# A two-layer graph attention kernel: a new order on all engines, and the value bias rows as pairs of 32-row matmuls

## The chip, the cores and the metric

The kernel runs on one core of one Trainium2 chip. The time is the device time of one execution in microseconds (us). The kernel before took 2665.45 us in the median of 3 runs (2662.31 to 2666.25).

## What is computed

The input is `x` (128 graphs, 128 nodes, 256 features, fp32) and `adj` (128 x 128 x 128, int32). Two layers follow each other, each with 8 heads of 32 columns:

```
# layer 0
q, k = x @ Wq + bq, x @ Wk + bk
attn = softmax(q k^T / sqrt(32))
out  = sum over r in 0..3 of (attn * (adj == r)) @ (x @ Wv[r] + bv[r])
x    = ln(x + out @ Wo + bo) * g1 + beta1
x    = ln(x + gelu(x @ W1 + b1) @ W2 + b2) * g2 + beta2
# layer 1 (no biases on q, k, v)
e    = leaky(q k^T);  attn = softmax(where(adj > 0, e, -9e15))
out  = ln(attn @ v) * g1 + b1
out  = ln(concat(out, x) @ Wffn^T) * g2 + b2
return out + x
```

The value biases `bv[r]` (4 x 256 = 1024 numbers) are one of the two things that the change touches.

## The kernel before, in words

**Pairs.** Two graphs are worked on at a time, a pair: 64 pairs in all. Every product of two fp32 matrices is made of three fp16 products (high x high, high x low, low x high). So each operand is split by a copy on ScalarE (ACT) that makes the high part and a subtraction on VectorE (DVE) or GpSimd (POOL) that makes the low part.

**Stages of one pair on TensorE (PE).** Named by their functions: `transpose_x`, `queries_keys_0` (12 matmuls of 256 columns each for q and for k), `values_0` (four jobs `v0_0` to `v0_3`, each a bias matmul and 6 matmuls of 512 columns), `scores` of layer 0 (`s0`: 16 fp32 matmuls of 32 rows, four row groups of the array into four banks, recorded as 32), `transpose_edges`, `attend_0` for each graph (64 small matmuls), `transpose_attention_0`, `output_projection` (y0), `transpose_x1` (yT0), `hidden` (four jobs of 12 matmuls), `feed_forward` (f, 48 matmuls), `transpose_x2` (xT1), `queries_keys_1`, `scores` of layer 1 (`s1`: four 512-column matmuls that put the mask down, then 16 fp32 matmuls in row groups), `values_1` (v1), `attend_1`, `transpose_attention_1` (oT1) and `last_product` (w, 24 matmuls).

**The bias.** `bv_rows` has 128 partitions, all zero but two: row 0 holds the high part of all 1024 biases and row 32 the low part. In `values_0` (L473) one matmul of `ones16` (128 x 128) with 512 columns of `bv_rows` starts each of the four banks (L478), and the six products are added to it. That is four bias matmuls for each pair.

**The order.** It is written out by hand. Each engine has a function `steps(n)` (PE L599, ACT L802, DVE L1030, POOL L1187, and L403 for the DMA queue of SyncE) that `pipeline` calls for n = 0 to 68. In step n an engine does, in a fixed order, stages of several pairs: `hidden(n - 2, 0)` is the hidden layer of the pair two behind. Every engine goes strictly through its list; semaphores (one for each result, counting up) hold it where an input isn't there or a buffer isn't free. PE's list before begins with f(n-3), v1(n-4), y0(n-2), v0_1 and v0_2(n-1), w(n-5), xT1(n-3), v0_3(n-1), k1(n-3), yT0(n-2), edges(n-1), q1(n-3), the hidden jobs (n-2), and ends with xT0(n), attend_0(n-1, 0), s1(n-3), attend_1(n-4), attend_0(n-1, 1), q0, k0, v0_0 and s0(n), oT0(n-1), oT1(n-4). What follows calls the work between two such calls a step; a full step has all of them.

**Banks.** All results of PE go through the eight banks of PSUM. `PE_BANKS` (L29) gives in PE's order the job, its bank, its lag, and the semaphore that says that the bank has been read out. `bank_free` makes a job wait for the reader of the job before it in the same bank.

**DMA.** SyncE loads x and adj (adj twice), transposes the probabilities of both layers (`transpose_probs_0`, `transpose_probs_1`) and stores the result. The store reads `x2b`. POOL writes `x2b` twice for a pair: `residual_shift_1` (L1172) puts x2 + b2b there and `result` (L1180) adds the normed rows. `residual_shift_1(m)` waits until the store of pair m - 1 has landed (L1177), and in POOL's list before it comes soon behind the `result` of that pair, with two instructions between (L1114 and one L1151); behind it on POOL stand `hidden_low` 1 and 2, `rstd("o1")` and `attention_scaled_0`, for which PE's oT0 waits.

Of the kernel before, what the change touches and what calls it, by code (L numbers as in the profile page):

```python
# [6 lines left out]
F16 = mybir.dt.float16  # L7
# [6 lines left out]
P = 128  # L14
G = 2
# [13 lines left out]
PE_BANKS = [  # L29
    ("f", 2, 3, "f_added", 1, 1),  # L30
    ("v1", 1, 4, "v1_lo", 1, 1),
    ("y0", 7, 2, "y0_added", 1, 1),
    ("v0_1", 2, 1, "v0_lo", 4, 2),
    ("v0_2", 0, 1, "v0_lo", 4, 3),
    ("w", 3, 5, "w_normed", 1, 1),
    ("xT1", 7, 3, "xT1_lo", 1, 1),
    ("v0_3", 5, 1, "v0_lo", 4, 4),
    ("k1", 7, 3, "k1_sb", 1, 1),
    ("yT0", 4, 2, "yT0_lo", 1, 1),
    ("edges", 6, 1, "p0_masked", 4, 4),  # L40
    ("q1", 0, 3, "q1_sb", 1, 1),
    ("h_0", 4, 2, "h_gelu", 4, 1),
    ("h_1", 2, 2, "h_gelu", 4, 2),
    ("h_2", 5, 2, "h_gelu", 4, 3),
    ("h_3", 4, 2, "h_gelu", 4, 4),
    ("xT0", 7, 0, "xT0_lo", 1, 1),
    ("o0_0", 3, 1, "o0_added", 2, 1),
    ("s1_0", 2, 3, "s1_leaky", 4, 1),
    ("s1_1", 1, 3, "s1_leaky", 4, 2),
    ("s1_2", 4, 3, "s1_leaky", 4, 3),  # L50
    ("s1_3", 5, 3, "s1_leaky", 4, 4),
    ("o1_0", 6, 4, "o1_scaled", 2, 1),
    ("o1_1", 0, 4, "o1_scaled", 2, 2),
    ("o0_1", 7, 1, "o0_added", 2, 2),
    ("q0", 2, 0, "q0_sb", 1, 1),
    ("k0", 3, 0, "k0_sb", 1, 1),
    ("v0_0", 7, 0, "v0_lo", 4, 1),
    ("s0_0", 1, 0, "p0_lo", 4, 1),
    ("s0_1", 0, 0, "p0_lo", 4, 2),
    ("s0_2", 6, 0, "p0_lo", 4, 3),  # L60
    ("s0_3", 4, 0, "p0_lo", 4, 4),
    ("oT0", 3, 1, "oT0_lo", 1, 1),
    ("oT1", 5, 4, "oT1_affine", 1, 1),
# [27 lines left out]
def build(nc, a, out):  # L91
# [12 lines left out]
    with ExitStack() as ctx:  # L104
# [1148 lines left out]
```

## Time and profile before

| what | value |
|---|---|
| median of 3 runs | 2665.45 us |
| the profiled execution, first to last instruction | 2664.5 us |
| PE busy | 2484.1 us (93%) |
| ACT busy | 2271.1 us (85%) |
| DVE busy | 2100.7 us (79%) |
| POOL busy | 1914.5 us (72%) |
| mean granted clock of PE | 0.982 of full speed |

The span leaves out only what lies around the first and the last instruction; it is 0.95 us under the median. A busy share is that of the whole span, so it doesn't say what ends a wait. Matmuls are pipelined and their ends are modelled: of two neighbouring rows on PE, the difference of the starts is the measure. The rows of the timeline merge neighbouring instructions of one kind (x12 is twelve); a bracket gives idle time before the row and what ended it.

### The profile page before, as it was taken

What the parts mean: (1) busy time and instruction counts of PE and PEld (TensorE: products, weight loads), DVE (VectorE), ACT (ScalarE), POOL (GpSimd) and SP (SyncE); (2) the same over time, 40 slices, a digit from 0 to 9 for tenths busy, and PEclk for the clock granted to TensorE, in tenths of its full rate; (3) what the DMA queues carried; (4) which work ended last, traced back from release to release, by engine and by line L of the source; (5) the groups of instructions that cost most, each with busy time, mean ns of one, the idle gap of its engine ahead of it and who ended that gap; (6) DMA issues with size and microseconds to landing.
All of it is one profiled execution on the core that took longest, in us unless ns stands there. A gap on an engine that the chain in (4) does not pass through costs nothing.

```text
span 2664.5 us, 83008 instructions
## 1 busy us (share of the span) xinstructions
PE 2484.1 (93%) x31496; PEld 1991.9 (75%) x31496; DVE 2100.7 (79%) x3730; ACT 2271.1 (85%) x6226; POOL 1914.5 (72%) x2126
## 2 busy tenths in 40 slices
PE   2799999999999999999999999999999999999974
PEld 1577777778777777777777877877777777777763
DVE  4578888888888878878888888888888888787842
ACT  3588998998898888898899899889989988888963
POOL 1358778777777867777877777787777777677764
PEclk9899999999999999999999999999999999999986
DMA  4134424424433433433442443343344334244222
GB/s 130 33 57 89 75 59 89 83 60 80 89 68 66 89 68 66 89 68 66 89 83 56 84 89 65 69 89 74 60 89 83 65 75 83 54 86 83 57 55 44
DMA packets 610377, 196.72 MB, mean 74 GB/s; under 512 B 539072, under 2 KB 609216, under 8 KB 609984
## 3 DMA queue, kind: packets, MB, share of 16 engines
q1 hardware_dynamic: 606816, 188.01, 36.5%
q8 instruction: 254, 4.16, 0.7%
q10 hardware_dynamic: 3168, 3.41, 0.5%
q14 instruction: 139, 1.14, 0.1%
HBM read 40.38 MB, written 16.78 MB: 21 GB/s over the span
## 4 chain that ended last, share of the span: by engine, by line
PE 42%; POOL 16%; ACT 16%; issue 11%; DVE 10%; DMA 2%; POOLq 0%; ACTq 0%; SPq 0%; DVEq 0%
PE bank L432 28%; PE bank L516 7%; ACT bank L699 4%; ACT p L688 3%; POOL x L1160 2%; ACT L688 2%; PE bank L449 2%; POOL x L1162 2%; PE bank L497 2%; DMA out_dram<-x2b 2%; ACT oT_f L792 2%; PE bank L490 2%; ACT k L708 2%; POOL y_rs L1123 2%; POOL p1h L1166 1%
## 5 line engine op out<-in xcount | busy, mean ns | idle before, releaser
L931 DVE TENSOR_TENSOR pm<-pT,bank 128x4096 f16<-128x4096 f16 x256 | 567.6, 2278 | 2.5 <-DMA pT<-p0h 2.5
L432 PE MATMUL bank<-wv,xT 128*128 128x512 f16 (+1 forms) x2304 | 471.0, 345 | 6.0 <-DVE p0h L886 1.9
L432 PEld LDWEIGHTS bank<-wv,xT 128*128 128x128 f16 x2304 | 222.7, 98 | 189.1 <-DVE p0h L886 18.3
L432 PE MATMUL bank<-w,h 128*128 128x256 f16 x3072 | 355.3, 277 | 0.0
L432 PE MATMUL bank<-yT,w 128*128 128x256 f16 x3072 | 346.1, 273 | 6.3 <-DVE yT L886 0.8
L699 ACT ACTIVATE bank<-bank,p_nmax 128x128 f32<-128x128 f32 x1024 | 347.3, 340 | 1.3 <-DVE p_nmax L915 1.3
L432 PEld LDWEIGHTS bank<-yT,w 128*128 128x128 f16 x3072 | 296.5, 98 | 54.5 <-DVE yT L886 20.4
L432 PEld LDWEIGHTS bank<-w,h 128*128 128x128 f16 x3072 | 305.4, 99 | 39.1
L688 ACT ACTIVATE p<-p,p_nmax 128x128 f32<-128x128 f32 x1024 | 326.3, 397 | 4.3 <-DVE p_nmax L901 3.6
L1151 POOL TENSOR_TENSOR h<-h_f,h 128x512 f16<-128x512 f32 x256 | 297.5, 1174 | 5.5 <-ACT h L675 5.5
L1166 POOL TENSOR_TENSOR p1h<-p,p1h 128x512 f16<-128x512 f32 x256 | 291.2, 1159 | 6.5 <-ACT p1h L729 6.5
L886 DVE TENSOR_TENSOR p0h<-bank,p0h 128x512 f16<-128x512 f32 x256 | 172.7, 675 | 143.0 <-ACT p0h L773 143.0
L667 ACT ACTIVATE h_f<-bank,bff_col 128x256 f32<-128x256 f32 x512 | 209.8, 490 | 71.0 <-PE bank L432 71.0
L1099 POOL TENSOR_SCALAR edge_rows<-adj_i 128x256 f16<-128x256 int32 x256 | 214.0, 854 | 62.0 <-DMA adj_i<-in_adj_dram 58.1
L516 PE MATMUL bank<-v,pm 128*128 128x64 f16 (+1 forms) x8192 | 244.7, 184 | 7.1 <-DVE xT L886 4.7
L516 PEld LDWEIGHTS bank<-v,pm 128*128 128x128 f16 x8192 | 237.2, 96 | 8.7 <-DVE xT L886 5.1
L1170 POOL TENSOR_TENSOR oT<-oT_f,oT 128x512 f16<-128x512 f32 x64 | 74.0, 1156 | 220.8 <-ACT oT L800 220.8
L886 DVE TENSOR_TENSOR v<-bank,v 128x512 f16<-128x512 f32 (+1 forms) x384 | 218.1, 582 | 0.2 <-ACT v L735 0.2
L699 ACT ACTIVATION_READ_ACCUMULATOR bank<-bank,p_nmax 128x1 f32 x1024 | 212.5, 208 | 0.0
L432 PE MATMUL bank<-xT,wk 128*128 128x256 f16 x1536 | 191.3, 275 | 16.8 <-DVE xT L886 16.8
L432 PEld LDWEIGHTS bank<-xT,wk 128*128 128x128 f16 x1536 | 147.0, 98 | 63.5 <-DVE xT L886 45.9
L432 PE MATMUL bank<-xT,wq 128*128 128x256 f16 x1536 | 192.4, 276 | 1.4 <-DVE xT L886 1.4
(127 smaller groups left out, 5632.7 us busy)
## 6 DMA issues: line engine op xcount, KB each, us to landing
x_sb<-in_x_dram SPq DMA_DIRECT2D x64, 256.0 KB, 3.5
adj_i<-in_adj_dram SPq DMA_DIRECT2D x128, 128.0 KB, 3.1
out_dram<-x2b SPq DMA_DIRECT2D x64, 256.0 KB, 2.1
pT<-p0h SPq DMA_TRANSPOSE x128, 4.7
pT<-p1h SPq DMA_TRANSPOSE x128, 4.8
pm<-in_L_gnn_W_dram ACTq DMA_DIRECT2D x1, 1024.0 KB, 13.1
pm<-in_L_gnn_W_dram SPq DMA_DIRECT2D x1, 1024.0 KB, 16.5
h_f<-in_L_gnn_Wffn_dram SPq DMA_DIRECT2D x1, 512.0 KB, 10.5
```

Of the source, the lines that this page charges most:

```text
L432: last = nc.tensor.matmul(o, l, r, start=(first and k == 0), stop=(k == len(todo) - 1))
L449: last = nc.tensor.transpose(o[:, at:at + P], src[:, g, c * P:(c + 1) * P], ident[:])
L516: last = nc.tensor.matmul(to, pm0[g][:, s, r, hd], v, start=(r == 0 and s == 0), stop=(r == REL - 1 and s == 0))
L667: last = nc.scalar.activation(h_f[:, c], ps(f"h_{i}")[:, (c % 2) * T:(c % 2 + 1) * T], ACT.Gelu, bias=bff_col[:, c:c + 1])
L688: last = nc.scalar.activation(p1[:, r, g, c], p1[:, r, g, c], ACT.Exp, bias=p1_nmax[:, r, g, c:c + 1])
L699: last = nc.scalar.activation(ps(f"s0_{r}")[:, at:at + P], ps(f"s0_{r}")[:, at:at + P], ACT.Exp, bias=p0_nmax[:, r, g, c:c + 1], accum_out ...
L886: return V_.tensor_tensor(to, source, high, ALU.subtract)
L931: V_.tensor_tensor(pm0[g][:, s], pT0[g][:, s].unsqueeze(1).broadcast_to([P, REL, HEADS, P]), edges[:, g].unsqueeze(2).broadcast_to([P, REL ...
L1099: last = V_.tensor_scalar(edge_rows[:, :, r], adj0_i[:], float(r), None, ALU.is_equal)
L1151: V_.tensor_tensor(h[:, 1, 2 * i:2 * i + 2], h_f[:, 2 * i:2 * i + 2], h[:, 0, 2 * i:2 * i + 2], ALU.subtract).then_inc(S["h_lo"], 1)
L1166: V_.tensor_tensor(p1h[:, :, 1, :, r], p1[:, r], p1h[:, :, 0, :, r], ALU.subtract).then_inc(S["p1_lo"], 1)
L1170: V_.tensor_tensor(oT1[:, 1], oT1_f[:], oT1[:, 0], ALU.subtract).then_inc(S["oT1_lo"], 1)
```

## The change

**The bias rows.** `bv_rows` becomes 128 x 512. In each of the four row groups of 32 rows, row 0 holds the high part and row 1 the low part of 512 of the biases. ACT and DVE make both parts on partition 0, in the memory of `p0h` and `p1h`, and SyncE copies them into place with eight small DMAs in the first block. In the pair loop a bias matmul uses 32 rows of the array, and they are issued as pairs ahead of the products:

```diff
+                sp.wait_ge(s_const, CONSTANTS)
+                sp.wait_ge(s_lo, 2)
+                for i in range(ROWS):
+                    cols = slice(i % 2 * BANK, (i % 2 + 1) * BANK)
+                    sp.dma_start(bv_rows[i * DH:i * DH + 1, :], bv_hi[0:1, cols]).then_inc(s_bias, 16)
+                    sp.dma_start(bv_rows[i * DH + 1:i * DH + 2, :], bv_lo[0:1, cols]).then_inc(s_bias, 16)
+                sp.wait_ge(s_bias, 2 * 16 * ROWS)
...
+                def value_biases_0(m, jobs):
+                    for i in jobs:
+                        bank_free(f"v0_{i}", m)
+                    for i in jobs:
+                        rows = slice(i * DH, (i + 1) * DH)
+                        nc.tensor.matmul(ps(f"v0_{i}")[:], ones16[rows, :], bv_rows[rows, :], start=True, stop=False,
+                                         tile_position=(i * DH, 0))
+
                 def values_0(m, i):
                     g, cols = i // 2, slice(i % 2 * BANK, (i % 2 + 1) * BANK)
-                    bank_free(f"v0_{i}", m)
-                    pe.wait_ge(S["xT0_lo"], m + 1)
-
-                    nc.tensor.matmul(ps(f"v0_{i}")[:], ones16[:], bv_rows[:, cols], start=True, stop=False)
+                    x_transposed(m)
                     products(ps(f"v0_{i}")[:], rows_of(wv0, xT0, g, cols), first=False).then_inc(S["v0_ps"], 1)
```

**The order on PE**, whole, in place of the list at L599 to L646 (pairs are counted from 3 to 8 behind n, so the earliest stage of a pair, `transpose_x`, stands at n - 3):

```
q1(n-7) yT0(n-6) edges(n-5) k1(n-7) h_0 h_1 h_2(n-6) s1(n-7) h_3(n-6) attend_1(n-8, 0 and 1)
attend_0(n-5, 0) s0(n-4) xT0(n-3) attend_0(n-5, 1) f(n-6) biases(n-4, v0_0 and v0_1) oT0(n-5) v0_0(n-4)
oT1(n-8) v0_1(n-4) biases(n-4, v0_2 and v0_3) y0(n-5) v0_2 v0_3(n-4) w(n-8) xT1(n-6) v1(n-7) q0 k0(n-3)
```

The scores of a pair now come in the step after its q0 and k0, with all four value jobs, and its attention comes one step later still. In `scores_1` the four mask matmuls no longer wait for q1 and k1, only for the mask and the banks.

**The order on ACT** (its own count of n): probs_high_1(n-6, 2) exp_1(n-6, 3) x_high(n-2) probs_high_1(n-6, 3) values_high_0(n-3, 1) x2_high(n-5) values_high_0(n-3, 2) values_high_1(n-6) q0 out(n-2) values_high_0(n-3, 3) x1_high(n-4) k0 out(n-2) q1 and k1 out(n-5) last_rows_normed(n-7) gelu 0, high 0, gelu 1, gelu 2, high 1(n-4) leaky 0, 1, 2(n-5) gelu 3, high 2(n-4) leaky 3(n-5) high 3(n-4) exp_1(n-5, 0) attention_half_0(n-3, 0) exp_0(n-2, 0) attention_half_0(n-3, 1) probs_high_0(n-2, 0) exp_0(n-2, 1) exp_1(n-5, 1) probs_high_0(n-2, 1) probs_high_1(n-5, 0 and 1) exp_1(n-5, 2) attention_high_0(n-3) attention_affine_1(n-6) values_high_0(n-2, 0) attention_high_1(n-6) exp_0(n-2, 2 and 3) probs_high_0(n-2, 2 and 3).

**The order on DVE**: attention_added_0(n-3, 0) max_1(n-5, 2) attention_added_0(n-3, 1) normalize o1(n-6) probs_low_0(n-2, 0 and 1) residual_ff, statistics and aggregate f(n-4) attention_low_0(n-3) max_0(n-2, 3) max_1(n-5, 3) normalize f(n-4) values_low_0(n-2, 0) residual_0, statistics y0(n-3) recip_0, probs_low_0(n-2, 2) aggregate y0(n-3) probs_low_0(n-2, 3) x_low(n-1) normalize y0(n-3) statistics w(n-6) values_low_0(n-2, 1) x2_low(n-4) aggregate w(n-6) values_low_1(n-5) values_low_0(n-2, 2 and 3) x1_low(n-3) by_edge_type(n-2, four times) max_1(n-4, 0) recip_1, attention_scaled_1(n-5) no_edge(n-3) max_1(n-4, 1) statistics and aggregate o1(n-5) max_0(n-1, 0 to 2). The maxima of layer 0 and 1 were blocks of four; now they are single, each with a wait of its own.

**The order on POOL**: edge_types(n-1) rstd o1(n-5) residual_bias_ff(n-3) attention_scaled_0(n-2) probs_low_1(n-4, 0) residual_shift_1(n-5) probs_low_1(n-4, 1) rstd f(n-3) attention_low_1(n-5) x2_scaled, x2_shifted(n-3) rstd y0(n-2) probs_low_1(n-4, 2) x1_scaled, x1_shifted(n-2) probs_low_1(n-4, 3) rstd_shift_w, result_scaled(n-5) residual_bias_0(n) result(n-5) hidden_low(n-2, 0 to 3).

**The order of SyncE**: both transposes of the probabilities of layer 0 (n-2), load_adj0(n-1), both transposes of layer 1 (n-5), load_x(n), load_adj1(n-3), store(n-6). Before it was: the first transpose of layer 0 (n-1), load_x and load_adj0(n), the second transpose (n-1), both of layer 1 (n-4), store(n-5), load_adj1(n-2).

**The banks** follow the new order. The ones that matter below: s0 has banks 0, 4, 6 and 2, and bank 2 is freed by the first `attention_scaled_1` on DVE (`("o1_0", 2, 8, "o1_scaled", 2, 1)`); h has 4, 2, 3, 4; oT0 has bank 0 behind the scores s0_0; f has bank 5 behind the edges; v1 has bank 4 behind y0. No stage is added or left out, and no count of instructions changes but that of the bias rows' preparation.

## Rows read from the trace of the kernel before

**Rows 1.** The page: the span

```profile
span 2664.5 us, 83008 instructions
```

**Rows 2.** Busy time by windows: one step in mid run (us, busy and instructions; clock, DMA)

```profile
1240.78:1279.79 39.01, 38.32 (x495) 30.81 (x494) 32.64 (x59) 35.14 (x98) 29.87 (x34) 1.00 0.38 76
```

**Rows 3.** Timeline of PE, the same step: start, length, instructions, idle time before

```profile
1240.78 0.60 PE L449 MATMUL bank<-ident,x_sb 128*128 128x128 f32 x4
...
1242.95 1.02 PE L490 MATMUL bank<-neg_mask,ident 128*128 128x512 bf16 x4
1243.90 1.17 PE L497 MATMUL bank<-k,q 32*128 32x128 f32 x32
1245.01 1.38 PE L432 MATMUL bank<-v,pT 128*128 128x33 f16 x48
...
1253.30 0.65 PE L449 MATMUL bank<-ident,o 128*128 128x128 f32 x4
1254.26 0.63 PE L449 MATMUL bank<-ident,o 128*128 128x128 f32 x4 [0.32 <-DVE o L979]
1254.73 5.40 PE L432 MATMUL bank<-w,h 128*128 128x256 f16 x48
1260.23 1.48 PE L432 MATMUL bank<-wv,xT 128*128 128x256 f16 x12
...
1269.16 1.46 PE L432 MATMUL bank<-wv,xT 128*128 128x512 f16 x6
1270.80 1.47 PE L432 MATMUL bank<-xT,wk 128*128 128x256 f16 x12 [0.18 <-DVE xT L886]
...
1272.99 1.47 PE L432 MATMUL bank<-xT,wq 128*128 128x256 f16 x12
1274.55 5.40 PE L432 MATMUL bank<-yT,w 128*128 128x256 f16 x48
1279.79 0.60 PE L449 MATMUL bank<-ident,x_sb 128*128 128x128 f32 x4
```

**Rows 4.** Timeline of POOL and PE in a slow step; landing times of the stores

```profile
968.59 1.27 POOL L1178 TENSOR_TENSOR x2b<-x,b2b_row 128x512 f32<-128x512 f32 x1 [2.36 <-DMA out_dram<-x2b]
...
974.36 0.63 PE L449 MATMUL bank<-ident,o 128*128 128x128 f32 x4 [1.72 <-POOL o L1106]
...
976.55 6.54 PE L432 MATMUL bank<-w,h 128*128 128x256 f16 x48
...
DMA to landing us min/median/max: 2.1/2.1/4.5
```

**Rows 5.** Timeline of PE: the last four records of the score burst of rows 3

```profile
1244.79 0.29 PE L497 MATMUL bank<-k,q 32*128 32x128 f32 x4
```

**Rows 6.** Groups by line and shape, whole run: busy, mean ns, idle before

```profile
L931 DVE TENSOR_TENSOR pm<-pT,bank 128x4096 f16<-128x4096 f16 x256 | 567.6, 2278 | 2.5 <-DMA pT<-p0h 2.5
L979 DVE TENSOR_SCALAR o<-o,o_mv,o_rs 128x256 f32<-128x256 f32 x128 | 140.4, 1136 | 47.4 <-POOL o_rs L1123 47.2
L979 DVE TENSOR_SCALAR f<-f,f_mv,f_rs 128x256 f32<-128x256 f32 x128 | 47.1, 410 | 44.3 <-POOL f_rs L1123 44.3
```

**Rows 7.** Timeline: end of the first block (DVE), start and end of the pairs (PE)

```profile
33.89 0.68 DVE L293 TENSOR_TENSOR wv<-p,wv 128x512 f16<-128x512 f32 x1
...
46.05 1.17 PE L497 MATMUL bank<-k,q 32*128 32x128 f32 x32
...
71.19 2.74 PE L516 MATMUL bank<-v,pm 128*128 128x64 f16 x64 [2.23 <-DVE xT L886]
...
94.71 1.01 PE L449 MATMUL bank<-ident,x 128*128 128x128 f32 x4 [2.46 <-POOL x L1141]
...
191.03 5.40 PE L432 MATMUL bank<-w,h 128*128 128x256 f16 x48
...
2515.38 5.40 PE L432 MATMUL bank<-w,h 128*128 128x256 f16 x48
...
2638.76 0.84 PE L432 MATMUL bank<-v,pT 128*128 128x33 f16 x24 [7.54 <-DMA pT<-p1h]
```

More of the change, by code:

```diff
@@ L26 @@
 CONSTANTS = 10
+DEPTH = 8
 PE_BANKS = [
[L30 to L42, printed above, removed]
@@ L57 @@
[L57 to L63, printed above, removed]
+    ("q1", 6, 7, "q1_sb", 1, 1),
+    ("yT0", 2, 6, "yT0_lo", 1, 1),
+    ("edges", 5, 5, "p0_masked", 4, 4),
+    ("k1", 1, 7, "k1_sb", 1, 1),
+    ("h_0", 4, 6, "h_gelu", 4, 1),
+    ("h_1", 2, 6, "h_gelu", 4, 2),
+    ("h_2", 3, 6, "h_gelu", 4, 3),
@@ new lines @@
+    ("s1_0", 1, 7, "s1_leaky", 4, 1),
+    ("s1_1", 7, 7, "s1_leaky", 4, 2),
+    ("s1_2", 0, 7, "s1_leaky", 4, 3),
+    ("s1_3", 6, 7, "s1_leaky", 4, 4),
+    ("h_3", 4, 6, "h_gelu", 4, 4),
+    ("o1_0", 2, 8, "o1_scaled", 2, 1),
+    ("o1_1", 3, 8, "o1_scaled", 2, 2),
+    ("o0_0", 1, 5, "o0_added", 2, 1),
+    ("s0_0", 0, 4, "p0_lo", 4, 1),
+    ("s0_1", 4, 4, "p0_lo", 4, 2),
+    ("s0_2", 6, 4, "p0_lo", 4, 3),
+    ("s0_3", 2, 4, "p0_lo", 4, 4),
+    ("xT0", 7, 3, "xT0_lo", 1, 1),
+    ("o0_1", 3, 5, "o0_added", 2, 2),
@@ L64 @@
+    ("f", 5, 6, "f_added", 1, 1),
+    ("v0_0", 3, 4, "v0_lo", 4, 1),
+    ("v0_1", 1, 4, "v0_lo", 4, 2),
+    ("oT0", 0, 5, "oT0_lo", 1, 1),
+    ("oT1", 4, 8, "oT1_affine", 1, 1),
+    ("v0_2", 5, 4, "v0_lo", 4, 3),
+    ("v0_3", 0, 4, "v0_lo", 4, 4),
+    ("y0", 4, 5, "y0_added", 1, 1),
+    ("w", 3, 8, "w_normed", 1, 1),
+    ("xT1", 6, 6, "xT1_lo", 1, 1),
+    ("v1", 4, 7, "v1_lo", 1, 1),
+    ("q0", 2, 3, "q0_sb", 1, 1),
+    ("k0", 7, 3, "k0_sb", 1, 1),
 ]
 SEMAPHORES = {
-    "pe": ["xT0_ps", "edges_ps", "s1_ps", "h_ps", "o0_ps", "w_ps", "q0_ps", "k0_ps", "oT0_ps",
-           "f_ps", "s0_ps", "v0_ps", "y0_ps", "xT1_ps", "o1_ps", "q1_ps", "k1_ps", "v1_ps", "yT0_ps",
-           "oT1_ps"],
@@ L263, in _ @@
                     cols = slice(half * V // 2, (half + 1) * V // 2)
-                    for part in (0, DH):
-                        nc.scalar.activation(bv_rows[part:part + 1, cols], src[part:part + 1], ACT.Copy).then_inc(s_hi, 1)
+                    nc.scalar.activation(bv_hi[0:1, cols], src[0:1], ACT.Copy).then_inc(s_hi, 1)
                 for c in range(2 * KC):
@@ L334, in bank_before, with pipeline @@
                     return S[name], per * (n - back - lag) + k
-        def pipeline(steps, least, most):
-            for n in range(least, PAIRS + most):
+        def pipeline(steps):
+            for n in range(PAIRS + DEPTH):
                 steps(n)
@@ new lines, in steps @@
+                    if live(n - 6):
+                        hidden(n - 6, 0)
+                        hidden(n - 6, 1)
+                        hidden(n - 6, 2)
+                    if live(n - 7):
+                        scores_1(n - 7)
+                    if live(n - 6):
+                        hidden(n - 6, 3)
+                    if live(n - 8):
+                        attend_1(n - 8, 0)
+                        attend_1(n - 8, 1)
+                    if live(n - 5):
+                        attend_0(n - 5, 0)
@@ L972, in statistics, with normalize @@
                         V_.bn_aggr(mv[:, g], st[:, g]).then_inc(S[name + "_mean"], 1)
-                def normalize(name, rows, to, m):
+                def normalize(name, m):
                     _, mv, _, rs = ln[name]
@@ L1085, in _ @@
+                pipeline(steps)
             @block.gpsimd
```

636 lines of the change are left out of this document (339 added, 297 removed).

## The prediction

> **What bounds the kernel now.** The windows view of one step in mid run comes first [rows 2]. The reader should see that a step takes 39.01 us, that PE is busy for 38.32 of them, ACT for 35.14, DVE for 32.64 and POOL for 29.87, at full clock. So PE sets the pace, and ACT has 3.9 us to spare. The second view is PE's timeline of that step [rows 3]. Forty-eight matmuls of 256 columns start every 0.109 us (1274.55 to 1279.79); against this measure four places lose time:
> - oT0 starts at 1253.30 and oT1 at 1254.26. Four transposes take 0.44 and the way out of the score burst costs a little, so 0.47 are a wait for the normed o1.
> - f takes 48 x 0.109 = 5.23, so v1 could start at 1259.96; it starts at 1260.23, 0.27 late (its bank is read out by the low part of the probabilities).
> - Six matmuls of 512 columns are 12 x 0.109 = 1.31, but k1 starts 1.64 after v0_3's products: 0.33 for the low part of xT1.
> - The hidden layer starts 1.56 after q1, not 1.31: 0.25 for the low part of yT0.
>
> The sum is 1.32 us a step. The third view says that not all steps are like this one. Full steps (those with all stages, 5 to 63) begin with f at 191.03 and the first step after them at 2515.38 [rows 7]: 59 steps take 2324.35, a mean of 39.40. 59 x 39.01 would be 2301.6, so 23 us lie in slow steps. One of them shows why [rows 4]: POOL's write of x2b waits 2.36 us for the store of the pair before (stores land after 2.1 us in the median, but up to 4.5), what stands behind it is late, PE waits 1.72 us for oT0's input, and then its clock drops: f's 48 matmuls take 6.54 where they took 5.40. The last view is the two ends: 191.0 us before the full steps, 2664.5 - 2515.4 = 149.1 after them [rows 1, 7].
>
> **Part 1, bias rows: about nothing.** Removed are four matmuls of 512 columns, 4 x 0.218 = 0.87 us a step. Added are two pairs on 32 rows. What a pair costs is bounded by the score bursts, the only place where row groups are used now. Inside a burst four matmuls run side by side: its last four records and the next full matmul lie 0.22 apart (1244.79, 1245.01) [rows 5], though the seven gaps before, from 1243.90 to 1244.79, are 0.127 in the mean [rows 3, 5]. So leaving the row groups costs about 0.10. Entering costs 1243.90 - 1242.95 - 4 x 0.218 = 0.08 [rows 3]. A pair thus comes to 0.08 + 0.22 + 0.01 + 0.10 = 0.41; with fp32 transposes or a weight load that can't be pulled ahead behind it, up to twice the switches, 0.59; without any switch cost, 0.23. The change is 2 x 0.41 - 0.87 = -0.05, between -0.41 and +0.31. I take +0.03, since the first pair is followed by fp32 transposes, as one score burst is. The Trainium skill speaks against this part: its page "TensorEngine Tiling (Array Packing)", Key Properties, says that a change of the tiling mode drains the engine; the trace agrees, with the 0.08 and 0.10. Its page "TensorE: Matmul & The Clock Gate", part 3, has a span model without such a cost (the matmul plus 4 ns for each further tile); by it a pair would be near the lower bound.
>
> In the first block SyncE gets eight small DMAs behind ACT's and DVE's work on one row. That block ends with DVE's work on the weights at 34.57 (33.89 + 0.68) [rows 7], last in a long list that doesn't wait for the bias rows; the rows are issued when the first parts are made. Cost nothing; if the rows landed later than that, each us would count once.
>
> **Part 2, the waits on PE.** For each of the four I compare the work that now covers the chain.
> - oT1: its input took from the end of attend_1 (1245.01 + 1.38) to 1254.26, 7.9 us. In the new list attend_0, s0, xT0, attend_0, f, a bias pair, oT0 and v0_0 stand between. An attend_0 is 1242.95 - 1240.78 - 0.44 = 1.73 and a burst with its entry 1.11 + 0.08 = 1.19, so they are 1.73 + 1.19 + 0.44 + 1.73 + 5.23 + 0.41 + 0.44 + 1.31 = 12.5. Gone: -0.47.
> - v1's bank now is that of y0, read 5 us earlier. Gone: -0.27. Late next could be oT0, whose bank waits for the low part of the first scores: that came about 6.9 us after the burst (the wait of v1 at 1260.23 shows it), and 7.9 us of PE work now stand between.
> - k1 and q1: xT1 is followed by v1, q0 and k0, 3.9 us where v0_3 gave 1.5. Gone: -0.33.
> - hidden: before, edges and q1 lay between yT0 and it; now edges and k1, the same 1.75 us, with the same two instructions on ACT and DVE. The 0.25 stay.
>
> New waits would come from the other engines' queues. I put PE's new list on a clock of 38 us and each engine's list beside it, with the lengths of the step before. The narrowest places: s0 needs bank 2, which DVE frees behind x1_low, four masks of 2.28 [rows 6], a maximum, two reciprocals and a scaling. The masks are 9.1 and the rest, from yT0 on, about 3.5 (an estimate), 12.6 in all; PE's work from yT0 to s0 is 1.75 + 0.25 + 5.23 + 2.06 + 1.2 + 1.73 + 0.44 = 12.7. So it is just covered. s0's bank 6 waits for leaky 3 on ACT, y0 for the low part of oT0: some 0.5 to 0.9 of margin each. ACT's waits for PE (in front of x1_high, q0 out, the affine of oT1) come to about 3 us and its work to 35.1: just inside 38. normalize f now has POOL at work beside it, and there the trace has a price: 1.14 us each for o1, where POOL works, against 0.41 for f, where it waits [rows 6]. That is +1.5 us of DVE time, in front of xT1, whose margin is 1.5 to 2. I book +0.02 for all of these.
>
> A step then is 39.01 - 0.47 - 0.27 - 0.33 + 0.03 + 0.02 = 37.99.
>
> **Part 3, the slow steps.** residual_shift_1 moves to the next round of POOL's list: between `result` and it stand four low parts of h, four edge compares and more, some 12 us by estimate, where two instructions stood. Even a store that lands after 4.5 us no longer holds it. SyncE's store is now last in its list, behind the transposes of layer 1, which POOL's result needs more time than. Of the 23 us I book 3 as left over, for other chance delays.
>
> **Part 4, the ends.** At the start, s0 of pair 0 ran at 46.05 and its second attention at 71.19, for the chain of exp, transposes and masks takes this long; before, all that PE did with pair 1 stood behind it, x for pair 1 too, since its load stood behind a transpose in SyncE's list. Now s0(0) comes at 45, then v0(0), xT0(1), q0 and k0(1) inside the chain, and load_x(1) is ahead of the transposes. I follow pair 0: attention until 74, y0 at 80, yT0 at 88 (94.71 before), f at 101, since nothing of pair 2 or 3 stands in front of it, q1 at 117. Those times are estimates from the chains of pair 0 before. 117 is the begin of step 4, which has 33.7 us of PE work (37.99 without attend_1, oT1 and w); full steps begin at 151, not 191.03. Bounds: 140 (chains as fast as the shortest seen) and 185 (as now). At the end, the last attend_1 came at 2638.76 behind a transpose of probabilities, 25.7 before the end, and PE hardly bounds: 149 before, and laid out in the new order 35 for step 64, then the chain of pair 63: 148. I take 149, between 142 and 165, because the new steps put a pair's w later in the step.
>
> **The sum.** 151 + 59 x 37.99 + 3 + 149 = 2544.4 for the span. The span was 0.95 below the median, so 2545.4.
>
> **The rivals.**
> 1. *The pairs cost no switch.* Then a step is 0.39 lower (2 x 0.23 - 0.87 = -0.41 in place of +0.03, less what s0's wait takes back): 2545 - 59 x 0.39 = 2522. For it: the records inside a burst start nearly together. Against: the 0.08 and 0.10. Chance 0.12.
> 2. *A queue on DVE or ACT binds.* The s0 chain has 0.1 us of margin by my layout and the slower normalize lies on the same engine. If it is late by 0.4 to 1.0 each step, the step takes 38.4 to 39.0: 2570 to 2605. Chance 0.20.
> 3. *The start isn't shorter.* Then +34 or +40: 2580. Against: the order of the lists. Chance 0.08.
> 4. *Slower.* PE waits for bank 2 by more than 2 us a step, because by_edge_type starts late (its transposes on SyncE or x1_low behind three value lows); then the clock falls in each step as in the slow ones, where f took 1.14 more [rows 4]. With a wait of 2 and 1.3 for the clock a step is 41.3: 151 + 59 x 41.3 + 3 + 149 = 2740. It decides from a step of (2664.5 - 303) / 59 = 40.03 on. For it: the same drop is in the trace. Against: DVE has 5 us to spare in a step. Chance 0.05.
>
> **How the numbers follow.** My forecast has 0.52. About 0.2% (5 us) is what a measurement of this kernel can tell from no change. Every case but the fourth lies over 60 us below 2665 except the upper edge of the second; the chances are 0.92 faster, 0.03 within, 0.05 slower. The range takes in the forecast with the bounds of the start and the pair, the first rival and most of the second and third: 2510 to 2600.
>
> **What would show it.** In the profile after: neighbouring xT0 37.9 to 38.1 us apart, with no group of steps at 40 to 42; no wait of POOL for the store; oT1, v1 and k1 directly behind their neighbours; hidden still 0.2 to 0.3 late; two bias matmuls starting nearly together, with 0.4 us between the full matmuls around them, and the first full step at about 151. It is wrong if PE waits before s0, if a bias pair takes 0.23 or 0.6 us, or if the first full step begins after 175.

## The result, and the profile after

The changed kernel takes 2529.64 us in the median of 4 runs (2528.23 to 2530.18), against 2665.85 for the kernel before on the same chip (2662.31 to 2667.03): a ratio of 0.9492, 95% interval 0.9478 to 0.9505. The prediction was 2545 (2510 to 2600). It is faster, as forecast, by 15 us more than forecast.

The page of the changed kernel, its span and busy shares (the mean granted clock of PE is 0.991 of full speed, 0.982 before):

```profile
span 2528.3 us, 83141 instructions
...
PE 2430.5 (96%) x31496; PEld 1984.4 (78%) x31496; DVE 2122.6 (84%) x3730; ACT 2212.6 (88%) x6224; POOL 1925.9 (76%) x2126
```

PE is busy for 54 us less and ACT for 59 us less; DVE has 22 and POOL 11 us more. PE's idle time falls from 180 to 98 us, so 83 of the 136 us of span are its waits. (The 133 more instructions are not in these counts: PE, DVE and POOL have as many as before, and ACT two fewer.) The windows view of one step in mid run (us, busy and instructions of PE, PEld, DVE, ACT, POOL; clock, DMA):

```profile
1203.10:1240.77 37.67, 37.67 (x495) 30.88 (x494) 32.84 (x59) 34.30 (x98) 30.06 (x34) 1.00 0.40 79
```

Against the step of before [rows 2] PE is now busy for all of it, and the step with its 495 matmuls takes 1.34 us less. The timeline of PE in that step (start, length, instructions, idle time before):

```profile
1207.46 1.48 PE L459 MATMUL bank<-xT,wq 128*128 128x256 f16 x12
1208.77 0.60 PE L476 MATMUL bank<-ident,x 128*128 128x128 f32 x4
1209.21 0.61 PE L496 MATMUL bank<-ident_h,edge_rows 128*128 128x128 f16 x8
1209.65 1.47 PE L459 MATMUL bank<-xT,wk 128*128 128x256 f16 x12
1210.96 4.09 PE L459 MATMUL bank<-yT,w 128*128 128x256 f16 x36
...
1219.49 1.89 PE L563 MATMUL bank<-v,pm 128*128 128x64 f16 x64
1221.31 1.17 PE L526 MATMUL bank<-k,q 32*128 32x128 f32 x32
1222.42 0.66 PE L476 MATMUL bank<-ident,x_sb 128*128 128x128 f32 x4
...
1224.65 5.40 PE L459 MATMUL bank<-w,h 128*128 128x256 f16 x48
1229.98 0.39 PE L511 MATMUL bank<-bv_rows,ones 32*128 32x512 f16 x2
1230.30 0.66 PE L476 MATMUL bank<-ident,o 128*128 128x128 f32 x4
1230.79 1.46 PE L459 MATMUL bank<-wv,xT 128*128 128x512 f16 x6
1232.09 0.60 PE L476 MATMUL bank<-ident,o 128*128 128x128 f32 x4
...
1233.92 0.39 PE L511 MATMUL bank<-bv_rows,ones 32*128 32x512 f16 x2
1234.24 1.48 PE L459 MATMUL bank<-wo,oT 128*128 128x256 f16 x12
```

No row has a bracket, and the starts leave no room for a wait too short to get one: oT1 (1232.09) starts 1.30 after v0_0's products (1230.79), its length; k1 (1209.65) and hidden (1210.96) follow their neighbours by 0.44 and 1.31, and v1 (1203.53) follows xT1 by 0.44. The three places of [rows 3] that were forecast to go are gone, and the fourth, hidden's 0.25, is gone too. Counted over the run, neighbouring f (and xT0) stand 37.67 apart in all but four of the full steps, and those four are 37.74 to 37.85: the slow steps of 40 to 42, which the kernel before has, are gone.

The ends, on the same timeline: s0 and yT0 of pair 0, q1 at the head of step 4, at that of step 5 (the first full one), and at that of step 64:

```profile
45.70 1.17 PE L526 MATMUL bank<-k,q 32*128 32x128 f32 x32 [1.02 <-ACT k L763]
...
88.31 0.63 PE L476 MATMUL bank<-ident,x 128*128 128x128 f32 x4 [0.55 <-POOL x L1225]
...
118.31 1.47 PE L459 MATMUL bank<-xT,wq 128*128 128x256 f16 x12
...
152.44 1.47 PE L459 MATMUL bank<-xT,wq 128*128 128x256 f16 x12
...
2375.63 1.47 PE L459 MATMUL bank<-xT,wq 128*128 128x256 f16 x12
```

So the account of the 136.2 us of span is: start 191.03 - 152.44 = 38.6; 59 full steps 2324.35 - 2223.19 = 101.2; end 149.1 - (2528.3 - 2375.6) = -3.6. Of the 101.2, the ordinary steps, 39.01 to 37.67, make 59 x 1.34 = 79, and the slow steps that are gone the other 22.

The two ends are counted here from where each list has its full steps, and the new list has f 17 us into a step. Counted by one event in both kernels, the f of pair 2 (191.03 before, 169.62 now) and the f of pair 61 (2515.38 and 2392.34), the start gives 21.4, what lies between 101.6 and the end 13.2. That the three waits of oT1, v1 and k1 are gone is read from the timeline; no run puts one of them back alone.

### The profile page after: what moved, and what is told of

It is laid out like the page before. It is cut to its first block and busy times, and to the rows that moved or that the text cites. A ratio compares the mean times of both kernels' runs of the same rounds, so it can differ in the third digit from the quotient of the medians.

```text
span 2528.3 us, 83141 instructions
## 1 busy us (share of the span) xinstructions
PE 2430.5 (96%) x31496; PEld 1984.4 (78%) x31496; DVE 2122.6 (84%) x3730; ACT 2212.6 (88%) x6224; POOL 1925.9 (76%) x2126
## 5 line engine op out<-in xcount | busy, mean ns | idle before, releaser
L459 PE MATMUL bank<-wv,xT 128*128 128x512 f16 (+1 forms) x2304 | 456.6, 344 | 0.0
L459 PE MATMUL bank<-yT,w 128*128 128x256 f16 x3072 | 356.8, 273 | 1.2 <-DVE yT L944 1.2
L754 ACT ACTIVATE bank<-bank,p_nmax 128x128 f32<-128x128 f32 x1024 | 353.9, 364 | 4.4 <-DVE p_nmax L968 4.3
L459 PE MATMUL bank<-w,h 128*128 128x256 f16 x3072 | 347.3, 273 | 2.8 <-POOL h L1172 2.8
L743 ACT ACTIVATE p<-p,p_nmax 128x128 f32<-128x128 f32 x1024 | 336.0, 437 | 1.3 <-DVE p_nmax L961 0.6
L459 PEld LDWEIGHTS bank<-w,h 128*128 128x128 f16 x3072 | 296.5, 98 | 37.4 <-issue 2.9
L1172 POOL TENSOR_TENSOR p1h<-p,p1h 128x512 f16<-128x512 f32 x256 | 296.6, 1159 | 30.5 <-ACT p1h L784 30.4
L754 ACT ACTIVATION_READ_ACCUMULATOR bank<-bank,p_nmax 128x1 f32 x1024 | 238.1, 232 | 0.0
L1268 POOL TENSOR_TENSOR w_n<-w_n,g2b_row 128x512 f32<-128x512 f32 x64 | 81.6, 1274 | 187.8 <-ACT w_n L837 187.8
L1040 DVE TENSOR_SCALAR o<-o,o_mv,o_rs 128x256 f32<-128x256 f32 x128 | 152.4, 1230 | 54.1 <-POOL o_rs L1204 54.1
```

The source lines that it names most:

```text
L459: last = nc.tensor.matmul(o, l, r, start=(first and k == 0), stop=(k == len(todo) - 1))
L743: last = nc.scalar.activation(p1[:, r, g, c], p1[:, r, g, c], ACT.Exp, bias=p1_nmax[:, r, g, c:c + 1])
L754: last = nc.scalar.activation(ps(f"s0_{r}")[:, at:at + P], ps(f"s0_{r}")[:, at:at + P], ACT.Exp, bias=p0_nmax[:, r, g, c:c + 1], accum_out ...
L1040: V_.tensor_scalar(rows_in(name, g), rows_in(name, g), mv[:, g, 0:1], rs[:, g:g + 1], ALU.subtract, ALU.mult).then_inc(S[name + "_normed"], 1)
L1172: return V_.tensor_tensor(to, source, high, ALU.subtract)
L1268: V_.tensor_tensor(w_n[:], w_n[:], both(g2b_row), ALU.mult).then_inc(S["out_scaled"], 1)
```

## The experiments

Twelve kernels were run, each beside the kernel before. Ratios are to that kernel, with a 95% interval.

**1. The bias part undone (full-array matmuls, in the new order).** A `ones16` with one block of 32 rows for each job takes the place of the row group:

```diff
-                        rows = slice(i * DH, (i + 1) * DH)
-                        nc.tensor.matmul(ps(f"v0_{i}")[:], ones16[rows, :], bv_rows[rows, :], start=True, stop=False,
-                                         tile_position=(i * DH, 0))
+                        nc.tensor.matmul(ps(f"v0_{i}")[:], ones16[:, i], bv_rows[:], start=True, stop=False)
```

> The kernel after, with each bias matmul again on all 128 rows of the array (the ones are 1 in one row group and 0 elsewhere), at the same places in the order. My theory (row groups run side by side, but entering and leaving them costs about 0.08 to 0.10 us each): a pair costs 2 x 0.216 = 0.43 in place of 0.41, and the transposes behind the first pair no longer lose 0.06; so no difference, 2528 to 2532. Rival (the new form pays as two matmuls for the price of one): 64 x 2 x 0.2 = 26 us slower, 2555.

Measured: 2529.88 us (2528.97 to 2531.18), ratio 0.9494 (0.9479 to 0.9508), steps of 37.64. The timeline of PE:

```profile
1223.52 5.40 PE L463 MATMUL bank<-w,h 128*128 128x256 f16 x48
1228.76 0.59 PE L514 MATMUL bank<-bv_rows,ones 128*128 128x512 f16 x2
1229.19 0.60 PE L480 MATMUL bank<-ident,o 128*128 128x128 f32 x4
```

Two full matmuls take 1229.19 - 1228.76 = 0.43, two side by side (above) 1230.30 - 1229.98 = 0.32 from start to next, and 0.09 more before them (f to the burst is 5.33, here 5.24). The bias part is worth nothing; all of the gain is the order's (that of all engines, with its banks and waits).

**2. Four single bursts in place of two pairs.**

```diff
+                        value_biases_0(n - 4, (0,))
                         values_0(n - 4, 0)
...
+                        value_biases_0(n - 4, (1,))
                         values_0(n - 4, 1)
-                        value_biases_0(n - 4, (2, 3))
```

(and the same for 2 and 3; the pair `(0, 1)` ahead of oT0 goes.)

> The kernel after, with the four bias matmuls on 32 rows issued one by one, each directly ahead of its own six products: four switches in and out for each pair of graphs, in place of two. My theory: each costs 0.08 + 0.22 + 0.10 = 0.41, four 1.64 in place of 0.88, 64 x 0.76 = 49 us slower: 2578, if nothing hides it. Rival (the pair takes 0.41 because its two matmuls stream one after the other, without a switch cost): 4 x 0.216, no difference: 2530.

Measured: 2603.44 us (2602.44 to 2604.15), ratio 0.9769 (0.9754 to 0.9784), steps of 38.86. PE's timeline:

```profile
1228.81 0.66 PE L476 MATMUL bank<-ident,o 128*128 128x128 f32 x4 [0.17 <-DVE p0h L947]
1229.40 0.39 PE L511 MATMUL bank<-bv_rows,ones 32*128 32x512 f16 x1
1229.71 1.47 PE L459 MATMUL bank<-wv,xT 128*128 128x512 f16 x6
```

A single matmul in a row group takes the 0.31 to its successor that a pair took (0.32), and behind other products the same 0.09 before it. So the two added bursts cost 0.82. The step grew by 1.19; the rest is a wait of oT0 for its bank, held by the low part of the first scores: the pair had stood ahead of it and hid 0.41 of that time. The expectation, 2578, had no such wait and was 25 us short; it was the wait that the prediction called "late next".

**3. Each pair issued twice (the bias is added twice in the result).**

```diff
-                    for i in jobs:
+                    for k, i in enumerate(jobs + jobs):
```

> The kernel after, with each pair of bias matmuls issued twice in one burst (the bias is added twice). My theory (side by side): the second pair costs one matmul more, 0.22, so 64 x 2 x 0.22 = 28 us slower: 2557. Rival (one after the other): 64 x 2 x 0.43 = 55 us slower: 2585.

Measured: 2557.85 us (2557.30 to 2558.57), ratio 0.9598 (0.9581 to 0.9615), steps of 38.11. Two more pairs add 0.44 a step, 0.22 each: what one matmul of 512 columns takes. Inside a burst two matmuls do run side by side; way in and way out are paid once for a burst.

**4. In the kernel before, POOL's shift of x2 made later.** It goes from behind `hidden_low(n - 2, 0)` to behind `attention_scaled_0(n - 1)`:

```diff
                         hidden_low(n - 2, 0)
-                    if live(n - 4):
-                        residual_shift_1(n - 4)
...
                         attention_scaled_0(n - 1)
+                    if live(n - 4):
+                        residual_shift_1(n - 4)
```

> The kernel before, with one change: residual_shift_1 stands last in POOL's list instead of between the low parts 0 and 1 of the hidden layer, so some 10 us more lie between it and the store that it waits for. My theory (the slow steps come from stores that land late): all steps take 39.0, the 20 to 23 us of slow steps are gone, 2643 to 2646, and POOL no longer waits for the store. Rival (the slow steps have another cause): 2664 to 2667.

Measured: 2646.79 us (2646.23 to 2651.45), ratio 0.9936 (0.9919 to 0.9953). Its waits view has no wait of POOL for the store (the kernel before has 17 of them, 26.8 us in all), and all its full steps are 39.00 to 39.33; 58 intervals between full steps take 2264.1, a mean of 39.04 where the kernel before has 39.39. The slow steps come from this one wait, and they are 21 us of the steps. By the medians (2664.24 beside it) the move gives 17 us. The execution in the profile is the slowest of its four, with 3.3 us more at the start and 2.2 us more at the end than the profiled one of the kernel before.

**5. The copy of yT0's high part on ACT put behind two others**, behind q1 out and k0 out:

```diff
+                    if live(n - 5):
+                        queries_keys_out_1(n - 5, "q1", q1)
+                    if live(n - 2):
+                        queries_keys_out_0(n - 2, "k0", k0, bk_col)
                     if live(n - 4):
                         x1_high(n - 4)
-                    if live(n - 2):
-                        queries_keys_out_0(n - 2, "k0", k0, bk_col)
-                    if live(n - 5):
-                        queries_keys_out_1(n - 5, "q1", q1)
```

> The kernel after, with ACT's x1_high (the high part of yT0) behind the copies of q1 and k0 instead of ahead of them: it should start about 0.8 us later, while PE's work between yT0 and the hidden layer stays 1.75. My theory (the 0.25 us that the hidden layer lost before was ACT's other work ahead of x1_high, not PE's cover): the hidden layer starts 0.7 us late in each step, 64 x 0.7 = 45 us slower: 2575. Rival (only PE's work in between decides): 2530.

Measured: 2571.91 us (2571.00 to 2572.78), ratio 0.9646 (0.9632 to 0.9661), steps of 38.36. PE's timeline:

```profile
1229.45 1.47 PE L459 MATMUL bank<-xT,wk 128*128 128x256 f16 x12
...
1231.45 4.09 PE L459 MATMUL bank<-yT,w 128*128 128x256 f16 x36 [0.53 <-DVE yT L945]
```

Hidden starts 2.00 after k1, not 1.31, and 0.69 is what the step grew by: the wait is back, by ACT's order alone, with PE's order as it is.

**6. In the kernel before, x loaded first on SyncE**, ahead of the first transpose of the probabilities:

```diff
                 def steps(n):
+                    if live(n):
+                        load_x(n)
                     if live(n - 1):
...
-                        load_x(n)
                         load_adj0(n)
```

> The kernel before, with SyncE's load_x(n) ahead of the transpose of layer 0's probabilities, as in the new order. My theory (the shorter start comes from PE's order, where q0 and k0 of the next pair stand ahead of the attention): 0 to 4 us faster, 2660 to 2664, the first full step still at 187 to 191. Rival (the late load of x made the long start): 20 to 39 us faster, 2626 to 2645.

Measured: 2668.07 us (10 runs, 2663.42 to 2672.24), ratio 1.0003 (0.9993 to 1.0013). It is not faster. The x of pair 1 is transposed at 59.47 (62.71 before), yet the first full step begins at 193.2. The load of x was not what made the old start long. That is as far as the runs go: that PE's order (pair 1's work ahead of pair 0's chain, 191.03 [rows 7]) did, is argued from the two timelines and was not isolated.

**7 and 8. The scaling of o1 made late on DVE**, to put a wait ahead of s0. First behind `no_edge` and the second maximum of layer 1; then behind three more reductions of a constant as well, whose result isn't used:

```diff
-                    if live(n - 5):
-                        recip_1(n - 5)
-                        attention_scaled_1(n - 5)
                     if live(n - 3):
                         no_edge(n - 3)
...
+                        for k in range(3):
+                            V_.tensor_reduce(small[:, k], ident[:].unsqueeze(1).broadcast_to([P, 4, P]), AX_X, ALU.max)
+                        recip_1(n - 5)
+                        attention_scaled_1(n - 5)
```

> The kernel after, with no_edge and the second maximum of layer 1 ahead of recip_1 and attention_scaled_1 on DVE, so that bank 2 is freed 0.9 us later. The trace after shows 0.45 us between its release and the scores of layer 0. My theory (that chain is the next to bind, and what goes beyond the margin is lost each step): 0.45 us a step, 64 x 0.45 = 29 us slower: 2558. Rival (the wait is made good by later waits that get shorter): 2530 to 2535.

> As e9_scaled_late, with three more maxima (of a constant, into an unused tile) ahead of recip_1: bank 2 is freed 0.9 + 1.8 = 2.7 us later. My theory of the slower case (a wait of over 2 us in each step also lets the clock fall, as in the slow steps before, where f took 1.14 us more): 64 x (2.25 + 1.2) = 220 us slower, 2750. Rival (the clock holds): 64 x 2.25 = 144, 2674.

Measured, the first: 2565.97 us (2565.21 to 2569.58), ratio 0.9627 (0.9612 to 0.9641), steps of 38.27. DVE and PE in one of them:

```profile
1238.43 0.28 DVE L955 TENSOR_SCALAR neg_mask<-adj_i 128x256 bf16<-128x256 int32 x1
...
1239.23 0.27 DVE L1073 RECIPROCAL o_rsum<-bank 128x8 f32<-128x8 f32 x2
...
1237.89 1.89 PE L563 MATMUL bank<-v,pm 128*128 128x64 f16 x64
1240.32 1.17 PE L526 MATMUL bank<-k,q 32*128 32x128 f32 x32 [0.53 <-DVE o L1080]
```

`no_edge` and the maximum behind it put the reciprocals and the scaling 1239.23 - 1238.43 = 0.80 later. From attend_0's start to s0's it takes 2.43, where the changed kernel takes 1.82 (1219.49 to 1221.31): 0.61 more, which is the growth of the step too (the bracket, between modelled ends, has 0.53 of it). So s0's margin in the changed kernel is 0.19, small, as forecast (0.1).

The second: 2771.33 us (2769.00 to 2773.81), ratio 1.0394 (1.0379 to 1.0410), slower than the kernel before. PE's timeline in one step, and the windows view of 500 us (its next to last three numbers are clock, DMA share, GB/s):

```profile
1252.54 1.41 PE L527 MATMUL bank<-k,q 32*128 32x128 f32 x32 [2.31 <-DVE o L1081]
1253.88 1.11 PE L477 MATMUL bank<-ident,x_sb 128*128 128x128 f32 x4
1254.79 2.54 PE L564 MATMUL bank<-v,pm 128*128 128x64 f16 x64
1257.17 5.40 PE L460 MATMUL bank<-w,h 128*128 128x256 f16 x48
```

```profile
1000.00:1500.00 500.00, 472.00 (x5929) 388.26 (x5925) 405.28 (x735) 417.51 (x1167) 359.94 (x398) 0.95 0.36 71
```

Another 1.78 us of delay (the bracket goes from 0.53 to 2.31) cost 3.3 a step: steps are mostly 41.4 to 42.2, 41.6 in the mean. From s0 to f it takes 4.63, where the changed kernel needs 3.34 (1221.31 to 1224.65): 1.29 more. In this stretch (1252.5 to 1257.2) the granted clock is 0.64 of full speed, most of it at the lower of the two levels, 1.2 GHz; from the f before (1215.85) to 1248.30 it is 1.00. Over the steps between 400 and 2300 us the stretch from s0 to f takes 1.43 more in the mean, and f itself 0.09 more, so 1.5 of a step is work at a lower granted clock behind the wait, and 1.78 + 1.5 is the 3.3. The clock over the window is 0.95 of full speed. This is the fourth rival made to happen.

**9. The changed kernel with the POOL shift put back** behind the first low part of the hidden tile:

```diff
-                    if live(n - 5):
-                        residual_shift_1(n - 5)
...
                         hidden_low(n - 2, 0)
+                    if live(n - 4):
+                        residual_shift_1(n - 4)
```

> The changed kernel with the POOL's shift of x2 put back to its earlier place, right behind the low part of the hidden tile, as it was before the change. Theory (in the kernel before, that place made the shift wait for its store in some steps, and the wait reached the PE; in the changed kernel the shift would come about 9 us after its store is issued, against landings of 2.1 to 4.5 us, and the POOL has slack): ordinary steps stay at 37.7, time 2530 to 2540. Rival (the order of the POOL as such is worth a share of the gain, each step): steps of 38.0 or more, 2550 or more.

Measured: 2628.08 us (2626.68 to 2631.18), ratio 0.9858 (0.9844 to 0.9871). My expectation was wrong by 90 us. POOL and PE:

```profile
1214.47 1.27 POOL L1273 TENSOR_TENSOR x2b<-x2b,w_n 128x512 f32<-128x512 f32 x1
...
1219.60 1.27 POOL L1264 TENSOR_TENSOR x2b<-x,b2b_row 128x512 f32<-128x512 f32 x1 [2.74 <-DMA out_dram<-x2b]
```

```profile
1231.84 0.66 PE L476 MATMUL bank<-ident,o 128*128 128x128 f32 x4 [1.70 <-DVE p0h L944]
1232.33 2.13 PE L459 MATMUL bank<-wv,xT 128*128 128x512 f16 x6
```

The 9 us between store and shift that I had counted weren't there: `result` ends at 1215.7, one low part lies between, and the shift waits for its store in each step (63 times, 115 us in all). What stands behind it on POOL, the statistics of o1, comes late; DVE's normalize and, queued behind that, the low part of the first scores come late; oT0 finds its bank taken. The quietest steps are 38.36, others 39 to 42, with a low clock again (0.68 of full speed from 1231.84 to 1237.10; six matmuls in 2.13, not 1.46). So the rival was nearer: the old place of the shift on POOL cost 17 us before (run 4) and costs 98 in the new order.

**10. The transposes of x ahead of the first scores**, with their line in `PE_BANKS`:

```diff
-                    if live(n - 4):
-                        scores_0(n - 4)
                     if live(n - 3):
                         transpose_x(n - 3)
+                    if live(n - 4):
+                        scores_0(n - 4)
```

> The changed kernel with one pair of neighbours on the PE swapped: the transposes of x that open a pair now stand ahead of the 32 matmuls of the first scores, not behind them. What this asks: the first-scores burst of the changed kernel is followed by transposes that begin about 0.06 us later than after a burst of full matmuls. Theory (the gap belongs to the end of a row-group burst, wherever it is, so it moves along to whatever follows): no gain, 2530 us, unless the operation behind it hides it. Theory two (it is the transposes behind the burst that pay, and behind products it is smaller): 64 times 0.04 to 0.06 us saved, 2526 to 2527. Rival (the first scores now come 1.1 us later against what they wait for and what waits for them, the second transposes of o or the probabilities' products): steps of over 37.9, 2545 or more.

Measured: 2531.09 us (2529.36 to 2533.88), ratio 0.9493 (0.9480 to 0.9506), steps of 37.66. The time is that of the first theory, but its reason doesn't hold. Over the steps between 400 and 2300 us, attend_0 behind the burst takes 1.75, where it takes 1.74 behind the transposes in the changed kernel, so 0.01 is all that it loses. The transposes ahead of the burst take 0.56 to its start, which is their 0.44, the way in of 0.09 that a burst has behind other matmuls, and 0.04 more. So fp32 transposes lose at the edge of a burst on either side of it, 0.06 behind and 0.04 ahead. The start hides something too: the first full step begins at 155.12, 2.7 later than in the changed kernel (152.44).

**11. The same, and the first x loaded in the opening block**, beside the weights, with the value bias staged in the memory of y0 and x1:

```diff
+                sp.dma_start(x_sb[0][:], x_d[0:G].rearrange("g t d -> t g d")).then_inc(S["x_in_0"], 16)
```

> The kernel of the run before (transposes of x ahead of the first scores), and the first group of x is loaded in the opening block, beside the weights, with the value bias staged in other tiles. Theory (the PE's first transposes of x wait for that load, which now stands behind the opening block): the start is some 2 to 3 us shorter and the rest the same, 2.7 below the run before, 2524 to 2527. Rival (the opening block lasts as long, bound by its weights, and x's load beside them only lengthens it): the same time as the run before or up to 1 us more.

Measured: 2526.34 us (2524.76 to 2530.49), ratio 0.9480 (0.9467 to 0.9493). The transposes of x for pair 0 start at 35.40, not 37.86, and all of f's starts are 2.9 earlier than in run 10, as expected. But that takes back little more than what run 10 had lost there: the first full step begins at 152.18, 0.3 earlier than in the changed kernel. It is the fastest kernel run, but its interval and that of the changed kernel overlap.

**12. All four bias matmuls in one burst.** On PE:

```diff
-                        value_biases_0(n - 4, (0, 1))
...
                         transpose_attention_0(n - 5)
...
                         transpose_attention_1(n - 8)
                     if live(n - 4):
+                        value_biases_0(n - 4, (0, 1, 2, 3))
+                        values_0(n - 4, 0)
                         values_0(n - 4, 1)
-                        value_biases_0(n - 4, (2, 3))
```

> The changed kernel with its four bias matmuls in one burst, one in each row group, behind f, oT0 and oT1, in place of two pairs. For that the second and third banks of the values change (v0_2 to 7, v0_3 to 5, k0 to 0), the transposes of x go behind y0 (bank 0), DVE makes the first low part of the probabilities while it would wait for the reciprocal root of o1, and the first x is loaded in the opening block, as in the run with the transposes of x first. Theory (the way into and out of the row groups is paid once for a burst, 0.20 us, and 4 matmuls side by side take what one does, 0.22): a burst of four costs 0.42, as a pair does, so 0.41 of each step goes. The work between f and the burst is 0.88 where f's bank needs about 0.8 to be read, and oT1's bank comes free about 0.15 after oT0, so 0 to 0.25 comes back: steps of 37.3 to 37.5 where the two changed kernels had 37.66, 2505 to 2517. Rival (row groups take turns beyond two, or f's bank or the nearer x1 and s0 chains bind): the burst costs 0.6 or more, or a wait of over 0.4 stands ahead of it or of s0; steps of 37.66 or more, 2526 or more.

Measured: 2533.35 us (2529.35 to 2535.96), ratio 0.9499 (0.9485 to 0.9514), steps of 37.70. PE and DVE:

```profile
1228.25 5.40 PE L460 MATMUL bank<-w,h 128*128 128x256 f16 x48
1233.64 1.32 PE L477 MATMUL bank<-ident,o 128*128 128x128 f32 x8
1234.99 0.40 PE L512 MATMUL bank<-bv_rows,ones 32*128 32x512 f16 x4
1235.32 2.76 PE L460 MATMUL bank<-wv,xT 128*128 128x512 f16 x12
```

```profile
1233.57 0.68 DVE L942 TENSOR_TENSOR p0h<-bank,p0h 128x512 f16<-128x512 f32 x1
1234.17 0.68 DVE L1058 TENSOR_TENSOR f<-bank,x1b 128x512 f32<-128x512 f32 x1
```

The steps of 37.3 to 37.5 that were expected didn't come; the time is the rival's. Half of the theory holds: four matmuls in four row groups take 0.33 to the next, where two took 0.32, so one burst of 0.41 is saved. The rest doesn't: from f's end (1228.25 + 5.23 = 1233.48) to the burst lie 1.51, where eight transposes and a way in take 0.98. The 0.5 of waiting stands in three small pieces without a bracket: oT0 0.16 late, behind POOL's scaling of o; oT1 behind the second low part (DVE, 1234.25); the burst behind f's bank, which DVE reads until 1234.85. Gain and waits cancel. With the transposes of x still ahead of f, the first of them might be covered; that wasn't tried.

## Why the prediction was right, and where it was off

**The sum.** Forecast span 2544.4, measured 2528.3: 16.1 less. By its terms: start 152.44 for 151 (+1.4); steps 37.68 for 37.99 in the mean (59 x -0.31 = -18.2); left over from slow steps 0 for 3 (-3); end 152.7 for 149 (+3.7).

**The steps.** The step of the sum that failed is "the 0.25 stay", for the hidden layer, and with it the sign "hidden still 0.2 to 0.3 late" and the 37.9 to 38.1 between neighbours. I compared the work on PE that covers the chain (the same 1.75 us) and took "the same two instructions on ACT and DVE" for the same time. But in the kernel before ACT came to them late, out of a full queue, and in the changed one it is waiting for them. PE's yT0 and ACT in the kernel before, then ACT in the changed one:

```profile
1272.10 0.60 PE L449 MATMUL bank<-ident,x 128*128 128x128 f32 x4
...
1272.62 0.58 ACT L751 ACTIVATE k<-bank 128x512 f32<-128x512 f32 x1
1273.09 0.59 ACT L766 ACTIVATE yT<-bank 128x512 f16<-128x512 f32 x1
```

```profile
1209.41 0.60 ACT L821 ACTIVATE yT<-bank 128x512 f16<-128x512 f32 x1 [1.73 <-PE bank L476]
```

Before, yT0 began at 1272.10 and ACT took it 0.99 later, behind a copy of k; now it takes it 0.64 after 1208.77. That is 0.35 earlier, enough for the 0.25. Run 5 shows it from the other side. Of the other 0.06 of the 0.31, 0.02 was booked for queues, and no such wait came. The rest is what the four gaps and the slow steps were read short by; it was not traced further.

**The bias pairs**: 0.41 each was forecast from the score bursts [rows 3, 5], and 0.41 it is. The +0.03 a step is what run 1 shows too (37.67 against 37.64), and in the median the two kernels are 0.24 us apart, less than can be told. The Trainium skill's page "TensorEngine Tiling (Array Packing)", Key Properties, which speaks of a drain when the mode changes, was the right warning; the span model of its page "TensorE: Matmul & The Clock Gate", part 3, by which a pair would be near 0.23 (an estimate), has no term for the 0.09 before and the 0.10 behind a burst. The first rival (no switch cost) falls with it.

**oT1, v1 and k1** went as forecast, each directly behind its neighbour. **Late next** was named rightly: oT0's bank (runs 2 and 9). **normalize f** mostly escaped the slowdown that I had booked, and that is luck: less than 0.1 us decides. Groups by line and shape, against [rows 6]:

```profile
L1040 DVE TENSOR_SCALAR o<-o,o_mv,o_rs 128x256 f32<-128x256 f32 x128 | 152.4, 1230 | 54.1 <-POOL o_rs L1204 54.1
...
L1040 DVE TENSOR_SCALAR f<-f,f_mv,f_rs 128x256 f32<-128x256 f32 x128 | 51.4, 444 | 10.8 <-POOL f_rs L1204 10.5
```

It is 444 ns where I had reckoned with 1140; o1's are 1230. In mid run its two instructions start at 1234.39 and 1234.7, and POOL's subtraction for oT at 1234.83. In run 1, with the same order on every engine, the mean is 848 ns, and in run 10 it is 655, with both cases side by side:

```profile
1199.08 0.73 DVE L1040 TENSOR_SCALAR f<-f,f_mv,f_rs 128x256 f32<-128x256 f32 x2 [0.20 <-POOL f_rs L1204]
1199.49 1.34 POOL L1172 TENSOR_TENSOR oT<-oT_f,oT 128x512 f16<-128x512 f32 x1 [0.44 <-ACT oT L855]
...
1236.75 1.71 DVE L1040 TENSOR_SCALAR f<-f,f_mv,f_rs 128x256 f32<-128x256 f32 x2
1237.15 1.15 POOL L1172 TENSOR_TENSOR oT<-oT_f,oT 128x512 f16<-128x512 f32 x1 [0.44 <-ACT oT L855]
```

Where POOL starts more than 0.41 after the first of the two, they take 0.73 together; where it starts less than 0.40 after it, 1.56 to 1.71; at 0.40 and 0.41 both occur. The changed kernel has 57 pairs of the first kind and 5 of the second, run 1 has 2 and 59. The times of both kernels are the same, so the margin behind normalize f takes up the 0.8 to 1.0 us. The price was real, then, and that it reaches no wait of PE was booked rightly.

**The second rival** (a queue on DVE or ACT) fell, though s0's margin was no more than 0.19 (run 7).

**The slow steps** were laid to the right wait: run 4 takes them away with this one move. Their worth in the new order I had not weighed, and run 9 shows it: without the move 98 of the 136 us are lost.

**The start** was 1.4 us off (the head of step 4 at 118.3 for 117), and the third rival (not shorter) fell; what made it shorter is argued and not shown (run 6 rules out the load of x). **The end** was 3.7 too short, inside its bounds.

**The fourth rival** did not come, since s0 had its margin, but its price was sound: with s0 2.4 us late and 1.5 for the clock (against the 2 and 1.3 of the prediction), steps are 41.6 for 41.3, and the time is 2771 us for 2740 (run 8).

## What to carry to other kernels

When work is reordered, a chain's slack is the work between its ends less the time each engine's queue needs to reach it: look at whether the engine comes to the link idle or late, and not only at what covers it. A burst in row groups has a fixed price at its edges (here 0.41 against 0.22 for each full matmul, so it must hold three or more before it is cheaper; four were run, three were not), and the banks for it must be free at one time. A write that waits for a store belongs a long way behind the store in its queue, the more so the less slack the rest of the schedule has.

## What the hardware showed that was not expected

- A burst of one, two or four 32-row matmuls of 512 columns takes 0.31 to 0.33 us to the next instruction. With the 0.09 before it, measured for one and two, that is 0.41 in all, against 0.22 for one on the full array.
- Four fp32 transposes lose 0.06 us directly behind a burst and 0.04 directly ahead of one; small fp16 matmuls (attend_0) lose 0.01 behind it (run 10 against the changed kernel).
- A wait of 2.31 us on PE in each step brought 1.5 us of slow work behind it in the mean, at a granted clock of 0.64 in the stretch shown; with a wait of 0.53 the clock over 500 us was 1.00 (runs 8 and 7; the steps grew by 3.9 and 0.60).
- One DVE instruction on one shape takes 410 ns or about three times that, by whether a POOL instruction started before it: two of them take 0.73 or 1.6 to 1.7 us, and at an offset of 0.40 to 0.41 us between the starts both occur. Where DVE was first, POOL's subtraction behind it took 1.34, not 1.15 (run 10).
- `no_edge`, also one DVE instruction with a scalar, took 280 ns in the mean before, 622 in the changed kernel (0.61 at 1221.00, beside a POOL subtraction that ran from 1220.30 to 1222.62), and 322 in run 7, where it starts while POOL waits (1238.43, 0.28). That is 22 us of DVE time over the run.
